# A copy of the rows' numbers, low weight halves ahead of the sums, and a reordered change-over in a fused attention and expert-mixture kernel

## What is computed

```python
q_prime = relu(einsum('bhnd,fd->bhnf', q, Wqf))      # 16 heads of 16, 64 features
k_prime = relu(einsum('bhnd,fd->bhnf', k, Wkf)) * mask
kv = einsum('bhnf,bhne->bhfe', k_prime, v)
out = einsum('bhmf,bhfe->bhme', q_prime, kv) / (qk_sum + 1e-08)
x = x + out @ Wo.T + bo                               # x was layer-normalised for q
h = layernorm(x)
topk_w, topk_idx = top_k(softmax(h @ gate_w), 2)      # weights scaled to sum 1
y = (silu(h @ w1[e]) * (h @ w3[e])) @ w2[e]           # for each token's two experts e
x = x + sum of weight * y
```

## Time and profile before

| what | us |
|---|---|
| median of 3 runs | 473.63 |
| lowest and highest of them | 463.7, 842.09 |
| the profiled execution | 464.74 |
| its span, first to last instruction | 463.0 |
| TensorE busy in it | 428.7 |
| VectorE, ScalarE, GpSimd busy | 209.6, 230.9, 213.3 |

### The profile page before, as it was taken

How to read it: one execution, slowest core, us unless ns; L and a number is a source line. 1 busy time by engine, 2 the same in 40 slices (tenths; PEclk the granted TensorE clock), 3 DMA queues, 4 the chain that set the end, 5 groups by cost and what they waited for, 6 DMA issues and landing times.

```text
span 463.0 us, 12218 instructions
## 1 busy us (share of the span) xinstructions
PE 428.7 (93%) x3921; PEld 396.0 (86%) x3922; DVE 209.6 (45%) x582; ACT 230.9 (50%) x477; POOL 213.3 (46%) x209
## 2 busy tenths in 40 slices
PE   3899999999999999989999998999999999999970
PEld 3789988898988888979999898899999899999970
DVE  4457788758876784323233331333232333233220
ACT  3677777578865523745333732553272373333320
POOL 4424375657434641798321671482177177121121
PEclk9999999999999999999999999899999999999996
DMA  8644121462128448335731236118121121121121
GB/s 255 195 134 156 47 70 48 145 234 70 49 59 286 114 128 260 80 122 168 256 54 24 37 110 187 23 35 272 23 43 29 23 39 30 23 46 23 36 37 11
DMA packets 34523, 46.10 MB, mean 100 GB/s; under 512 B 3488, under 2 KB 29344, under 8 KB 34464
## 3 DMA queue, kind: packets, MB, share of 16 engines
q1 hardware_dynamic: 22304, 31.82, 20.6%
q0 software_dynamic: 6576, 8.82, 11.3%
q10 hardware_dynamic: 5584, 4.76, 3.7%
HBM read 32.63 MB, written 12.76 MB: 98 GB/s over the span
## 4 chain that ended last, share of the span: by engine, by line
PE 68%; DVE 9%; issue 6%; POOL 5%; DMA 4%; ACT 2%; ACTq 1%; POOLq 1%; DVEq 0%
PE bank L814 28%; PE twin L833 15%; PE bank L852 4%; DMA out_rows<-qf,x_all 3%; POOL w_lo L486 3%; PE twin L667 3%; PE bank L547 3%; PE bank L548 2%; PE bank L549 2%; DVE w_lo L1229 2%; PE bank L593 2%; PE twin L679 2%; PE bank L571 2%; PE twin L792 1%; PE bank L610 1%
## 5 line engine op out<-in xcount | busy, mean ns | idle before, releaser
L496 POOL DMA_INDIRECT out_rows<-qf,x_all x35 | 54.6, 1559 | 147.4 <-ACT qf L1054 111.7
L814 PE MATMUL bank<-w_hi,c_hi 128*128 (+1 forms) x280 | 106.4, 380 | 3.8 <-issue 2.0
L814 PE MATMUL bank<-w_lo,c_hi 128*128 (+1 forms) x280 | 103.0, 368 | 0.0
L833 PE MATMUL twin<-w_hi,kv_halves 128*128 (+1 forms) x490 | 95.2, 286 | 2.9 <-DVE kv_halves L1335 2.4
L1329 DVE TENSOR_TENSOR x_all<-bank,x_all 128x448 f32<-128x448 f32 x70 | 43.4, 623 | 97.3 <-ACT x_all L1073 97.2
L486 POOL TENSOR_TENSOR w_lo<-raw,w_hi x18 | 76.0, 4422 | 12.8 <-ACT w_hi L1066 10.1
L1335 DVE TENSOR_TENSOR kv_halves<-bank,kv_halves 128x512 fp32r<-128x512 f32 x66 | 38.6, 623 | 93.9 <-ACT kv_halves L1078 93.9
L833 PEld LDWEIGHTS twin<-w_hi,kv_halves 128*128 128x128 f32 x490 | 77.5, 188 | 3.7 <-DVE kv_halves L1335 2.6
L814 PE MATMUL bank<-w_hi,c_lo 128*128 (+1 forms) x280 | 79.9, 367 | 0.0
L1073 ACT ACTIVATE x_all<-bank 128x448 f32<-128x448 f32 x70 | 37.8, 544 | 80.6 <-PE bank L814 70.1
L833 PE MATMUL twin<-w_lo,kv_halves 128*128 (+1 forms) x245 | 68.7, 280 | 0.0
(11 more groups left out here) (219 smaller groups left out, 703.4 us busy)
## 6 DMA issues: line engine op xcount, KB each, us to landing
raw<-in_w SPq DMA_DIRECT2D x24, 896.0 KB
x_all<-bucket ACTq DMA_DIRECT2D x31, 129.0 KB, 2.1
raw<-in_ctxT SPq DMA_DIRECT2D x8, 256.0 KB, 2.9
out_rows<-x_all SPq DMA_DIRECT2D x8, 256.0 KB, 2.1
bucket<-pad_rows SPq DMA_DIRECT2D x13, 129.0 KB, 2.4
x_all<-in_x SPq DMA_DIRECT2D x2, 512.0 KB, 6.4
x_all<-bucket SPq DMA_DIRECT2D x6, 129.0 KB, 2.7
x_all<-in_x SPq DMA_DIRECT2D x1, 768.0 KB, 6.3
```

What stands on the lines that cost most here:

```text
L496: pool.indirect_dma_start(out=out, out_offset=bass.IndirectOffsetOnAxis(ap=x_in[:, v, D:D + 1].bitcast(U32), axis=0), in_=y[:, v, :], in_o ...
L814: last = nc.tensor.matmul(bank[b][:, 0:MC], stationary[:, k, :], w[:, bass.ds(at + (of + k * M + c * MC), MC)], start=(k == 0 and part == ...
L833: last = nc.tensor.matmul(bank[6][:, 0:D], stationary[:, k, :], w[:, bass.ds(at + (2 * W13 + k * D), D)], start=(k == 0 and part == 0 and ...
```

## The change

1. The row number and weight of each tile's rows get a place of their own, `meta` (128 x 4 x 2). ScalarE copies them there (`copy_meta`) right behind the high half of that tile's rows; the sum and y read them from there. A copy for tile t waits for the sum of tile t-4, as its place is then free. Loads wait for the copy (`meta_ready`) and no more for a sum.
2. GpSimd makes all three low parts of the next expert ahead of the sum, where one stood ahead of it and two behind.
3. In the attention stage, pairs 2 to 4, VectorE's division goes ahead of the second weight piece. In the last pair ScalarE's high attention half goes ahead of the exponents. Behind the stage VectorE's second normalisation of pair 6 goes behind the first product of tile 0 and the last division.
4. At the change-over the output products of tiles 1 and 2 move behind the transposes of tiles 3's and 4's rows, and ScalarE's y with them; in tiles 2 and 3 the second part of g goes to bank 5 instead of 6, so TensorE waits for the last ranks to be read ahead of it.

```diff
+        meta = sb("meta", [P, 4, 2])
...
+        def shared(t):
+            return isinstance(t, int) and t < 2
...
         def g_banks(t):
-            return ((bank[4], 0, 4), (bank[6 if early(t) else 5], 4, MB))
+            return ((bank[4], 0, 4), (bank[6 if shared(t) else 5], 4, MB))
...
-            sp.wait_ge(y_added, 16)
+            sp.wait_ge(meta_ready, 1)
             sp.dma_start(x_in[:, 0, :], bucket[2 * P:3 * P, :]).then_inc(x_in_loaded[0], 16)
...
-            sp.wait_ge(y_added, 16 * 2)
+            sp.wait_ge(meta_ready, 2)
...
-                pool.indirect_dma_start(out=out, out_offset=bass.IndirectOffsetOnAxis(ap=x_in[:, v, D:D + 1].bitcast(U32), axis=0),
+                pool.indirect_dma_start(out=out, out_offset=bass.IndirectOffsetOnAxis(ap=meta[:, v, 0:1].bitcast(U32), axis=0),
...
-                low_halves((0,))
+
+                low_halves((0, 1, 2))
                 add(t - 1, (u - 1) % 4)
-                low_halves((1, 2))
...
             hidden(2, 0)
-            output(1)
             rank(NPR - 1)
             hidden(2, 1)
             x_transposes(3, 3)
+            output(1)
+
+            pe.wait_ge(rank_read, NPR)
             g_transposes(2)
             hidden(3, 0)
-            output(2)
             hidden(3, 1)
             x_transposes(4, 0)
+            output(2)
             g_transposes(3)
-            pe.wait_ge(rank_read, NPR)
...
                 query_features(i, 2)
+                if i == NPR - 1:
+                    high_attention(i - 1)
                 if i >= 2:
                     exponents(i - 2)
-                high_attention(i - 1)
+                if i < NPR - 1:
+                    high_attention(i - 1)
...
-                if tile_live(t, -4):
-
-                    act.wait_ge(y_added, 16 * (t - 3))
+
+                act.wait_ge(meta_ready, t - 3)
                 act.dma_start(x_in[:, u, :], bucket[bass.ds(at, P), :]).then_inc(x_in_loaded[u], 16)
...
+            def copy_meta(t, v):
+
+                if tile_live(t, -4):
+
+                    act.wait_ge(y_added, 16 * (t - 3))
+                nc.scalar.copy(meta[:, v], x_in[:, v, D:ROW]).then_inc(meta_ready, 1)
...
                 evacuate_x(t + 1)
+                copy_meta(t + 1, (u + 1) % 4)
...
-                if 2 <= i <= 4:
-                    low_piece(0, 2 * i - 3)
                 if i >= 6:
                     low_piece(1, 2 * i - 11)
                 attend(i - 1)
+                if 2 <= i <= 4:
+                    low_piece(0, 2 * i - 3)
...
-            normalise2(NPR - 2)
             gates(0, 0)
             attend(NPR - 1)
+            normalise2(NPR - 2)
```

More of the change, by code:

```diff
@@ L189, in build @@
         x_in_loaded = [sem(f"x_in_loaded{i}") for i in range(4)]
+        meta_ready = sem("meta_ready")
         xT_done, x_hi_ready, x_lo_ready = sem("xT_done"), sem("x_hi_ready"), sem("x_lo_ready")
@@ L824, in output @@
                     pe.wait_ge(y_ready, t)
-                if early(t):
+                if shared(t):
                     pe.wait_ge(g_lo_ready, 2 * t + 2)
                 for k in range(MB):
-                    if not early(t) and k in (0, g_banks(t)[1][1]):
+                    if not shared(t) and k in (0, g_banks(t)[1][1]):
                         pe.wait_ge(g_lo_ready, 2 * t + (1 if k == 0 else 2))
@@ L844, in g_transposes @@
                             pe.wait_ge(x_lo_ready, 2)
-                        if t > 0 and i == 1:
+                        if t == 1 and i == 1:
                             pe.wait_ge(y_ready, t)
@@ L1053, in evacuate_y @@
                     act.wait_ge(y_added, 16 * (t - 3))
-                nc.scalar.activation(y[:, v, :], bank[6][:, 0:D], ACT.Copy, scale=x_in[:, v, D + 1:ROW]).then_inc(y_ready, 1)
+                nc.scalar.activation(y[:, v, :], bank[6][:, 0:D], ACT.Copy, scale=meta[:, v, 1:2]).then_inc(y_ready, 1)
             def high_halves(first, t, part, slot_free):
@@ L1097, in _ @@
             evacuate_x(0)
+            copy_meta(0, 0)
             silus(0, 0)
             evacuate_x(1)
+            copy_meta(1, 1)
             silus(0, 1)
@@ L1108, in _ @@
             evacuate_x(2)
+            copy_meta(2, 2)
             evacuate_x2(NPR - 1)
@@ L1112, in _ @@
             silus(2, 0)
-            evacuate_y(1, 1)
             silus(2, 1)
             evacuate_x(3)
+            copy_meta(3, 3)
+            evacuate_y(1, 1)
             high_g(2)
             silus(3, 0)
-            evacuate_y(2, 2)
             silus(3, 1)
             evacuate_x(4)
+            copy_meta(4, 0)
+            evacuate_y(2, 2)
             high_g(3)
```

## The result

The changed kernel takes 475.84 us (median of 6 runs, 470.5 to 479.0); the kernel before, run beside it, 469.89. The ratio is 1.0187, with a 95% interval from 1.0102 to 1.0273. Forecast were 465.4 us and a range of 459 to 471: the time lies outside, on the slow side. The interval lies above 1; whether the loss is over 2% it leaves open. The ratios leave out executions in the chip's slower state, the medians don't.

What follows compares the result with a forecast made beforehand. TensorE, busy 93%, was taken to bound the kernel. On the profiled 464.74 us, terms -1.9 - 0.35 + 0.55 - 1.2 + 4.2 - 0.6 = +0.7 gave 465.4 us, no change that can be told; range 459 to 471.

Steps and rivals of the forecast that it cites:

- The third load falls where nothing waited and nothing will: Expert stage's loop, third expert load: no wait expected from its new time, so no term in the sum.
- of the second only a gain: Second expert load in the loop: tile 17's load issued 0.6 us earlier; term -0.6, ends 0 and -0.8.
- Low halves and the chain to tile 11: Expert stage: low halves ready earlier, -1.2; sums behind expert loads delay tile 11's load, +4.2.
- Rival A: Gains stand, no new wait at tile 11, as a sum behind a load lands in 5.4 us: 459.4 us; chance 0.25.
- net 0: TensorE's clock: old drop after tile 16's gap gone, -1.8, one new after tile 11's wait, +1.8.
- Attention, -1.9 and -0.35: Attention stage: division before a weight piece closes TensorE gaps, -1.9; last pair and second normalisation, -0.35.
- rival D: Moved weight piece stays slow beside GpSimd, its wait reappears at the attention product; gain only -0.5: 466.8 us; chance 0.10.
- the maximum ends at 65.4: Attention stage: VectorE's maximum, behind the moved piece of 1.1 us, ends then, so the attention product needn't wait.
- TensorE's tail, +0.55: Change-over: moved output products fill gaps, -1.5, but new waits at rank(7), +1.15, and tile 4's transposes, +1.3.
- 35 copies, 0: ScalarE's new copies of row numbers, about 0.2 us each, fit its idle time; at most +0.2 in two late rounds.
- B: Sums served only after the whole expert load, landing in 11.8 us, delay several tiles: 478.8 us; chance 0.05.
- C: New code places bring ScalarE one more 5 us instruction-fetch pause per loop round: 467 to 474, say 469; chance 0.08.

Runs made afterwards that it cites:

- both release experiments: Changed kernel with the expert load signalled behind the sum, by the old shared signal or by a separate one: 467.46 us and 468.27 us.
- late release: Changed kernel, but GpSimd signals the expert load by a memset behind the sum, and TensorE takes the low halves by that signal too: 467.46 us, ratio 0.9975.
- signal of its own: Changed kernel, but a separate signal behind the sum releases the expert load; TensorE keeps the old signal for the low halves: 468.27 us, ratio 0.9995.
- old attention stage: Changed kernel with the attention stage's three orders (weight piece, exponents, second normalisation) put back as before: 477.19 us, ratio 1.0212.

## Why the prediction was wrong, by its steps

**The base.** The sum was made on 464.74, one profiled execution; the median beside the changed kernel was 469.89. So 5.15 of the 10.4 us between forecast and measurement are the base. The forecast said that "nothing in the trace speaks of that gap"; a part of it is the clock, which took 5.6 us from the profiled execution (mean clock 0.988) and 7.5 to 9.0 from the mean one (below). But from 469.89 the sum would give 470.6, and the measured time is 5.2 above that: the steps failed too.

**"The third load falls where nothing waited and nothing will", and of the second only a gain: this failed, and it decides.** The prediction followed what a *sum* suffers behind an expert load, and not what a *tile's load* suffers there. It gave tile 17's load a gain of 0.6, from a release of the expert load at 271.9, and didn't ask which load of ScalarE's would then stand directly behind it. That was tile 16's, issued at 272.12 before and so 0.2 us behind the forecast release, and tile 20's at the next expert load: 2.3 and 1.9 us of waiting and a clock drop after each. Between tiles 12 and 21 this makes +4.8 us (2.0 - 2.2 + 5.0) where -2.4 was forecast (-0.6 and the drop of 1.8 gone). The gap of 1.68 did go: the -2.2 from tile 16 to 18 is that term.

**Low halves and the chain to tile 11: right.** GpSimd's low halves for expert 3 began at 217.13; tile 7 stands 5.3 us later than before, so that is 211.8 on the old scale, for 212.2 forecast. Forecast for tiles 5 to 12 were -1.2 + 4.2 = +3.0; measured +1.9, as the wait was 2.48 (+0.64 at the next product) and not 3.9 to 4.7. On the old scale the load was issued at 233.0 for 234.1 forecast, as sum 6 started 0.7 earlier, and TensorE had it 2.1 us after its issue, for 2.3 to 3.1. The low halves' own gain also came: TensorE no longer waits at tile 7. Rival A is out. The mechanism is shown by both release experiments: put the expert load behind the sum and the wait is gone.

**The clock: "net 0" failed.** The mean granted clock of each run, as a share of full speed, lets two parts be told apart: time x clock, which grows with waits, and the rest, time x (1 - clock), which was not granted. Over all runs of a kernel, means:

| kernel | time x clock | rest |
|---|---|---|
| before (its 29 runs beside the last four kernels) | 461.0 | 7.6 |
| changed kernel | 464.5 | 10.5 |
| copy and low halves | 463.5 | 13.5 |
| low halves alone | 480.1 | 23.3 |
| late release | 460.4 | 7.4 |
| signal of its own | 459.6 | 8.3 |
| old attention stage | 465.3 | 13.0 |
| copy alone; again | 457.4; 456.9 | 7.5; 8.7 |
| copy and reordered change-over | 458.8 | 8.0 |
| copy and attention stage (6 runs, uncertain by 1) | 455.6 | 7.7 |
| all but the low halves' order; again | 458.0; 457.4 | 6.8; 6.9 |

Beside the other kernels that of before had 460.6 and 9.0, and 460.9 and 7.5. So of the changed kernel's loss some 3.5 to 4 us are waits and 1.5 to 3 us are clock; a late load is mostly paid for twice, as a wait and at 1.2 GHz. In the three kernels with copy and low halves unchanged, eight of nine such waits (1.6 to 2.8 us) came with a stretch of half clock during them or behind them; the one that didn't is tile 11's in the profile above. The eight experiments without a late load had no such stretch between 210 and 440 us. Why a wait of this size brings one is not shown.

**Attention, -1.9 and -0.35: the gaps moved to the place that rival D, given 0.10, had named, but not by its cause.** The division ran early and the piece took 1.08 us (D had it slow), both as forecast, and the transposes start in time. But 0.94 and 0.85 came back at the attention product. In pair 3, VectorE and ScalarE after the change:

```profile
66.95 0.17 DVE L1259 TENSOR_REDUCE neg_max<-bank 128x2 f32<-128x16 f32 x1 [1.63 <-remote]
...
66.13 0.60 ACT L947 ACTIVATE qf<-bank 128x512 f32<-128x512 f32 x1 [1.95 <-remote]
```

and ScalarE's same step before:

```profile
64.47 0.60 ACT L939 ACTIVATE qf<-bank 128x512 f32<-128x512 f32 x1 [0.43 <-PE bank L610]
```

It started 0.14 us after TensorE's last record for it before, and 1.7 us after it now; the maximum, 1.9 us after the logits' last record (65.04). The profile names no releaser it knows ("remote"). The step that failed is "the maximum ends at 65.4". TensorE's results came later than its modelled ends say, in each of these places where it ran on without the gap. Why is not shown, and the new order is not the only place of such a wait: four profiles with the old order have one of 1.80 to 1.86 us on ScalarE in the last pair. All seven profiles with the new order have this pair of waits, of 0.85 to 0.94 us. The sixth attention transposes start 80.3 to 80.8 us behind the first with the old order (mean of seven 80.7), 80.5 to 80.6 with the new: 0.1, not 1.9.

Whether the new orders gain elsewhere is open. Three pairs of kernels differ in them alone, and in each the new ones are ahead by time x clock: by 0.8 (changed kernel and old attention stage), by 1.3 to 1.8 (added to the copy) and by 0.8 to 1.4 (added to copy and change-over). That is about 1 us, most of it not visible up to the sixth transposes; the traces don't show where it lies.

The +4.0 at tile 0 is not the order. In the profile above 1.7 us of it are half clock (0.50 in 134 to 136, then 0.66), and 1.00 is the wait ahead of that at 131.13, for ScalarE's copy of the transposed rows. Half clock from about 132 on is in nine of fourteen profiled executions, four of seven with the old order and five of seven with the new; seven of the nine have that wait, of 0.99 to 1.08 us, and none of the five without the drop has one of that size for that copy. Without the drop tile 0 comes at 134.0 to 136.2, whichever the order. The profiled execution of before, on which the sum was built, happened to be free of it.

**TensorE's tail, +0.55: mis-sized.** The two forecast waits came at their size: 1.19 at the ranks (1.15) and 1.18 at tile 4 (1.3). A third, 0.87, at the transposes of tile 3's g behind it, ended by VectorE, was not foreseen. Tiles 0 to 5 took 48.5 to 49.6 us in the seven profiles with the new tail that kept full clock there and 47.2 to 48.0 in the five with the old one: about +1.2. The copy with the new change-over stands 1.4 to 1.9 us of time x clock above the copy alone.

**The copy: "35 copies, 0", and true only "in name" that loads wait for no sum.** It was the change's best part. Alone it gains 0.6% (0.9935 and 0.9940): without the sum's wait, tiles 16 to 18 take 17.6 us instead of 21.1, and the next round's pause, which the prediction had cost "the same as before", costs nothing (8.35 us from tile 25 to 26 instead of 9.63; in the changed kernel 8.34, most of its -1.7 behind tile 21).

**The other rivals.** B's 478.8 is near the measured time for a wrong reason: sums behind an expert load land in some 8 us, not 11.8. C wanted one more pause of 5 us on ScalarE per round; the changed kernel's profile has none of over 3 us in the loop.

## What to carry to other kernels

When an edit moves the *release* of a big transfer, list every small transfer that will be issued on any queue while the big one runs, not only the one the edit names. Here the low halves ahead of the sum made a loss of 1.5 to 2.1% (7% without the copy) as long as the 2.7 MB load was signalled ahead of a sum and a 129 KB load; signalled behind them, they left the kernel level with before (0.9975 and 0.9995), and with the old order of the low halves and the copy it was 0.6 to 1.1% quicker in five of six measurements. Price an idle gap of TensorE of 2 us with the clock it may cost, and don't build on one profiled execution's clock.

## What the runs showed of the hardware

- Seven tile loads, in four of the kernels, were issued 0.6 to 1.0 us behind an expert load; TensorE waited for each and had it 6.4 to 7.4 us after its issue. Three issued only 0.33 to 0.37 us behind one were there within 4.9 to 5.2 us, and the longest wait for them was 0.24. None issued 0.8 to 1.9 us ahead of one was waited for. By the Trainium skill (DMA: Bandwidth & Descriptors, Queues, rings and completion order) a DMA engine takes turns between queues packet by packet; as an estimate from that, two equal sharers would double the 2.3 to 3.1 us of the earlier trace rows to 4.6 to 6.2. The runs agree in kind, and the seven lie above it.
- Half clock came with nearly all waits for a late load (1.6 us and more), but with none of tile 7's nine waits of 1.5 to 1.6 us. Between runs of the kernel before it makes most of the spread: 465.28 us at a mean clock of 0.987, 474.92 at 0.970, while time x clock differs by 1.4 us.
- Closing two TensorE gaps of 0.9 us gave 0.1 up to the sixth transposes: ScalarE and VectorE went on only 1.7 and 1.9 us after the ends of TensorE's records where the gap had been closed, and ScalarE 0.14 us after where it had not.
